# Row numbers of the result scatters: converted on GpSimd, one column per scatter and a chunk ahead, instead of on VectorE

## What is computed

```python
x = _layernorm(x + attention(x), axis=-1)
logits = xt @ router_w.T                      # (8192, 8)
topk_vals, topk_idx = jax.lax.top_k(logits, 2)
g = jax.nn.sigmoid(topk_vals)
g = g / (g.sum(axis=-1, keepdims=True) + 1e-10)
for e in range(E):
    ge = jnp.sum(jnp.where(topk_idx == e, g, jnp.zeros_like(g)), axis=-1)
    h = jax.nn.silu(xt @ w_gate[e]) * (xt @ w_up[e])
    out = out + ge[:, None] * (h @ w_down[e])
x = _layernorm(x + out, axis=-1)
```

## Time and profile before

| what | us |
|---|---|
| median of 3 runs | 834.15 |
| the three runs | 832.1, 841.45, 834.15 |
| span of the profiled execution, first to last instruction | 835.0 |
| expert stage, about | 516 to 796 |
| final sum and layer norm, about | 796 to 835 |

### The profile page before, as it was taken

How to read it: one execution, slowest core, us unless ns; L and a number is a source line. 1 busy time by engine, 2 the same in 40 slices (tenths; PEclk the granted TensorE clock), 3 DMA queues, 4 the chain that set the end, 5 groups by cost and what they waited for, 6 DMA issues and landing times. The chain is left out here.

```text
span 835.0 us, 33045 instructions
## 1 busy us (share of the span) xinstructions
PE 686.4 (82%) x13242; PEld 530.5 (64%) x13242; DVE 507.7 (61%) x1624; ACT 364.6 (44%) x546; POOL 432.0 (52%) x482
## 2 busy tenths in 40 slices
PE   4789999999999999999999978876868878879400
PEld 1356766666666667666666657866857877879400
DVE  6737766767777776776777653554533544444366
ACT  2134445434444444444453434443444544555248
POOL 6622065455546546654654553555545555555545
PEclk9799999999999999999999987888978889989855
DMA  6892544464364445446444030322223222222187
GB/s 166 235 274 74 150 133 131 127 176 128 99 182 132 123 136 157 128 125 176 132 122 126 27 83 27 116 58 68 71 83 100 73 77 78 71 74 71 42 333 274
DMA packets 83575, 103.53 MB, mean 124 GB/s; under 512 B 15488, under 2 KB 70144, under 8 KB 83424
## 3 DMA queue, kind: packets, MB, share of 16 engines
q1 hardware_dynamic: 73344, 82.26, 33.6%
q0 software_dynamic: 8640, 17.84, 6.7%
q10 hardware_dynamic: 1440, 1.31, 0.5%
HBM read 60.12 MB, written 40.79 MB: 121 GB/s over the span
## 5 line engine op out<-in xcount | busy, mean ns | idle before, releaser
L295 POOL DMA_INDIRECT slots<-rows_sb,slot_at x128 | 128.5, 1004 | 145.0 <-PE o_ps L1271 78.4
L550 POOL DMA_INDIRECT results<-scaled_sb,result_at x142 | 136.1, 959 | 125.5 <-DVE scaled_sb L1071 91.1
L797 DVE TENSOR_REDUCE neg_max<-score_ps 128x16 f32<-128x1024 f32 x109 | 133.2, 1222 | 86.2 <-PE score_ps L1215 84.5
L691 ACT ACTIVATE prob<-scoret_ps 128x1024 f32<-128x1024 f32 x109 | 111.6, 1024 | 145.7 <-PE scoret_ps L1215 142.4
L1271 PE MATMUL o_ps<-v_sb,prob 128*64 128x18 f32 x2048 | 74.9, 212 | 4.2 <-issue 4.1
L724 ACT CAST w_slot<-wgu_sb 128x1024 fp32r x71 | 75.1, 1058 | 0.0
L1271 PEld LDWEIGHTS o_ps<-v_sb,prob 128*64 128x64 f32 x2048 | 70.7, 142 | 5.4 <-issue 5.0
L1225 PE MATMUL score_ps<-bias_hl,fold 128*128 128x512 f16 x218 | 66.6, 387 | 3.5 <-DVE neg_max L797 3.5
L1231 PE MATMUL scoret_ps<-bias_hl,fold 128*128 128x512 f16 x218 | 66.9, 389 | 0.3 <-ACT prob L691 0.2
L1285 PE MATMUL ctx_ps<-diag,o_sb 128*64 128x64 f32 x896 | 53.7, 237 | 14.9 <-DVE o_sb L812 8.2
L1395 PE MATMUL o_ps<-wd_sb,h_sb 128*128 x288 | 46.4, 313 | 22.4 <-DVE h_sb L1060 19.6
(11 more groups left out here) (186 smaller groups left out, 1604.7 us busy)
## 6 DMA issues: line engine op xcount, KB each, us to landing
stack<-scratch SPq DMA_DIRECT2D x32, 512.0 KB
blocks<-scratch SPq DMA_DIRECT2D x126, 128.0 KB
scratch<-qk_hl SPq DMA_DIRECT2D x120, 128.0 KB
xin<-slots SPq DMA_DIRECT2D x71, 130.0 KB
blocks<-results SPq DMA_DIRECT2D x16, 512.0 KB, 6.5
x_sb<-in_x SPq DMA_DIRECT2D x16, 256.0 KB
out<-y_sb SPq DMA_DIRECT2D x16, 256.0 KB, 4.0
results<-scaled_sb,result_at POOLq DMA_INDIRECT x142
```

Of the source, the lines that this page charges most:

```text
L295: nc.gpsimd.indirect_dma_start(slots, bass.IndirectOffsetOnAxis(ap=slot_at[:, k % 2, n:n + 1], axis=0), rows_sb[:, k % 2, n // TT, n % TT, ...
L550: pool.indirect_dma_start(results, bass.IndirectOffsetOnAxis(ap=result_at[s % RBUF][:, t:t + 1], axis=0), scaled_sb[:, s % RBUF, t, :], No ...
L691: act.activation(prob[:, (par + u) % 2, :], turned_scores(i, u)[:, :, :].rearrange("p b c -> p (b c)"), ACT.Exp).then_inc(exp_done, 1)
L797: dve.tensor_reduce(neg_max[:, par, :, v, :], ps[:, :, :].rearrange("p b (h k) -> p b h k", k=W), AX_X, ALU.max, negate=True).then_inc(max ...
```

## The change

DVE's conversion of both columns in `scale` is taken out. POOL converts instead, one column at a time: the columns of chunk 0 ahead of the scatters, and column t of chunk s + 1 right behind scatter t of chunk s. Before the first column of a chunk POOL waits until the chunk's rows are loaded and until the scatters that used the same `result_at` buffer, eight chunks back, have landed. Each conversion adds one to a new semaphore, `addressed`. `results_out(s)` waits for it ahead of its scatters, and SP's load into an `xin` buffer waits for it too, besides `scaled`.

```diff
+        addressed = sem("addressed")
...
                 def slots_in(s):
 
                     after(sp, scaled, s + 1 - XBUF)
+                    settle(sp)
+                    after(sp, addressed, HT * (s + 1 - XBUF))
                     settle(sp)
...
+                def addresses(s, t):
+
+                    if t == 0:
+                        pool.wait_ge(load_in[s % XBUF], 16 * (s // XBUF + 1))
+                        settle(pool)
+                        after(pool, result_out[s % RBUF], 16 * HT * (s // RBUF))
+                        settle(pool)
+                    pool.tensor_copy(result_at[s % RBUF][:, t:t + 1], xin[:, s % XBUF, t, DM + 1:DM + 2]).then_inc(addressed, 1)
+
                 def results_out(s):
 
                     pool.wait_ge(scaled, s + 1)
+                    settle(pool)
+                    pool.wait_ge(addressed, HT * (s + 1))
                     settle(pool)
                     for t in range(HT):
                         pool.indirect_dma_start(results, bass.IndirectOffsetOnAxis(ap=result_at[s % RBUF][:, t:t + 1], axis=0),
                                                 scaled_sb[:, s % RBUF, t, :], None).then_inc(result_out[s % RBUF], 16)
+                        if s + 1 < SLOT_CHUNKS:
+                            addresses(s + 1, t)
...
                 all_steps(pool, step)
+                for t in range(HT):
+                    addresses(0, t)
                 for s in range(SLOT_CHUNKS):
                     results_out(s)
...
                     y = (o_ps, ctx_ps)[s % 2]
-                    dve.tensor_copy(result_at[s % RBUF][:, :], xin[:, s % XBUF, :, DM + 1])
                     for t in range(HT):
```

## The result

The changed kernel took 807.77 us in the median (807.11 to 810.17), the kernel before beside it 833.12 us (826.85 to 841.45). The ratio is 0.972 (95% interval 0.968 to 0.975), so the change made it faster by 2.8%. The prediction was 834.0 us within 825 to 844, with 0.12 on faster by over 1%: it was wrong.

What follows compares the result with a forecast made beforehand. It took the expert stage as set by PE, with stalls running PE result, silu, h_sb, PE. Span 835.0 - 0.5 (DVE) + 0 (loads) + 0.4 (end) = 834.9; the runs' median lies 0.85 below the span, so 834.0 us, range 825 to 844.

Steps and rivals of the forecast that it cites:

- Step 1, DVE: DVE's queue in the expert stage: losing the conversion ahead of the scaling gains 0.5 us, between 0 and 5.0.
- Step 2, POOL's spacing: POOL's scatter queue: each added conversion costs 0.2 us in the mean, between 0 and 0.57.
- the contention that the text argued against: POOL and DVE sharing SBUF interfaces: by the skill's rule conversions would stretch; the prediction saw none in the trace.
- Step 2, the room that hides it: POOL's idle time waiting for scaled results: 0.58 us free per conversion before POOL becomes the bound.
- Step 3, loads: SP's loads of rows, now also waiting for POOL's conversions: 10.5 us in hand against 2 to 4, cost 0.
- Step 4, the end: Last two chunks' scatters in POOL's queue: two conversions make the end 0.4 us later, 0 to 1.2.
- A: Rival, slower: POOL's queue of scatters and conversions becomes the bound, deciding from 0.58 us per conversion; 845 us, chance 0.15.
- B: Rival, faster: DVE's 0.07 us per chunk shortens PE's stalls; 829 us, or 824 with less low clock; chance 0.15.
- D: Rival: PE's stalls, of unnamed cause, fall otherwise in time, either direction, up to 1%; within forecast's spread, no separate chance.

Runs made afterwards that it cites:

- e3: Kernel before, with only DVE's conversion moved later, so that it no longer stands ahead of the scaling: 830.21 us, ratio 1.000.
- a1: The changed kernel run again, beside a kernel before of 741.0 us: 787.12 us, ratio 1.064.
- e1: Kernel before, DVE's conversion kept, plus an idle POOL conversion behind each scatter and the wait for its signal; SP's loads don't wait for it: 811.58 us, ratio 0.978.
- e7c: Kernel before, with results written by SP's plain DMAs to consecutive rows instead of scatters, beside a kernel before of 836.75 us: 742.94 us, ratio 0.891.
- e2: e1, with SP's load of rows also waiting for POOL's idle conversions as in the changed kernel: 812.22 us, ratio 0.978.
- e4b: e4 run again, beside a kernel before of 741.0 us: 744.24 us, ratio 1.007.
- e4: The changed kernel with one POOL conversion of both columns between the two scatters, in place of two conversions: 828.70 us, ratio 1.003.
- e5c: e1 with both idle conversions of a chunk behind its second scatter, beside a kernel before of 836.75 us: 816.14 us, ratio 0.978.

## Why the prediction was wrong

**Step 1, DVE.** Right as far as the runs can tell. It said 0.5 us, as silu and not the scaling decides; e3 measured 1.000 (0.996 to 1.004), which is 3 us either way.

**Step 2, POOL's spacing: mis-sized.** It put the mean cost of a conversion at 0.2 us within 0 to 0.57. The operation was right (0.193 us median in a1; 29.1 us over 142 in the result), and so was an extra within a pair (0.07 against 0.13). Wrong was the wait for POOL's own fresh signal: I took 0.17 us from the wait of rstd for ve, and it leaves 0.76. The mean is (3.27 - 2.52) / 2 = 0.37 us. Scatters were 0.98 us long beside a conversion, 0.96 without, so the contention that the text argued against is 0.02 us at most.

**Step 2, the room that hides it: the step that failed.** "82.6 / 142 = 0.58 us is free per conversion before POOL becomes the bound" took POOL's idle time as spare. It was idle because PE's results were signalled late, and they were late because of POOL's scatters, as e1 and e7c show. POOL at 3.27 us a chunk did become the bound, though 0.37 is below 0.58; and with its scatters held to 0.61 a us, the stalls that had made the room went away: late signals from 137 to 44, POOL's wait for scaled results from 91.1 to 14.9 us. Why 0.61 is slow enough is the inference above.

**Step 3, loads.** It said 10.5 us in hand and no cost. After the change PE's transposes wait 14.6 us for rows; the reserve is used up ahead of 22 chunks, because POOL is behind and the loads follow it. e1 has no such wait on SP and takes the same time as e2, so the wait is the form that POOL's bound takes, not a cost of its own.

**Step 4, the end.** It gave 0.4 us, for a queue that is as short as before. POOL ends 20 us behind the last h_sb instead of 6.

**The rivals.** A (POOL becomes the bound, slower) had the mechanism. Without late signals it is all there is: 787 against 741 us. Its price was set too low, for it was counted from the room of step 2. B (faster through shorter stalls) had the sign, and part of the effect, 14 waits for h_sb down to 4 at a higher clock, but by the wrong cause: 0.07 us less on DVE gives nothing that e3 can tell. D said that the stalls could fall otherwise, by up to 1%, and named no cause; the gain was 2.8%. What I should have asked of the earlier trace rows is why ACT waited 3.99 us for an engine that shows no gap; the range of 825 to 844 took that as a fixed background, and the 25 us of the result lay in it.

"GPSIMD Engine Reference" of the Trainium skill, section 4.1 "Engine selection", advises VectorE for elementwise work. Where the kernel before takes 741 us the runs agree: moving the conversion to POOL costs 6.4% as the change does it (a1) and 0.7% in the form of e4b. Where it takes 833 us, the same change gains 2.8%.

## What to carry to other kernels

- Idle time of an engine is room only if its cause doesn't depend on that engine. Follow one stall to the instruction that releases it, and compare that instruction's end with the start of the waiting one. Here a signal 3.8 us behind the end of its matmul, with the producer busy, pointed at the real subject.
- Have the kernel before run beside every experiment, and be wary of a gain that a purely idle instruction also gives: here it is a slower queue that happened to help. Between the two conditions the sign changes (0.972 and 1.064), while e4's single conversion between the scatters is within 1% of the kernel before in both (1.003 and 1.007); it is the form to take if the conversion has to be on POOL.
- Put a small operation where its signal has time to arrive before it is waited for: on POOL it costs 0.07 us there and 0.68 (1.94 - 1.26) directly ahead of the wait.

## What the runs showed of the hardware

- The same program, the kernel before, took 829 to 837 us in three groups and 741 in two. Where it is slow, PE's signals come 1 to 12 us after the matmul's modelled end in the expert stage, and 29 to 38 of some 470 also in attention, from 100 to 480 us (0 to 2 of some 495 where it is quick), where the changed kernel loses 20 us more. A 4096-byte packet of a scatter of results takes 193 ns in the median in the kernel before and 193 ns in e4b, so these transfers aren't slower.
- In the slower condition the scatters of results bring the late signals of the expert stage (137 of 275 in the kernel before), and plain DMAs at a higher traffic don't (8 of 291 in e7c). Which resource signals of PE and scatters share is open, and so is what differs between the two conditions. The traces with late signals also hold fewer records of DMA signals (6,796 before, 7,114 changed; 10,981 in a1), so how much the recording itself has to do with it stays open too.
- The fastest time, 722 us with results by plain DMA, shows what scatters cost even where signals are on time: 740.7 - 722.3 = 18.4 us. It isn't a kernel to use, since its rows are not where they belong, and I found no kernel that beats both: 741 stays the best in one condition and the changed kernel's 808 in the other, where e1 (812) and e5c (816) lie near it.
